# A two-layer attention and expert network: a new planner with timed transfers, other buffers, and the low halves of gated values on POOL from the third dense pass on

## What is computed

```python
x = x + xattn0(layernorm(x), ctx)   # kv = ctx @ W_k.T + b_k; softmax(layernorm((p@kv) @ kv.T))
x = x + ffn0(layernorm(x))          # rms(dense gelu FFN) + rms(top-2 of 8 experts), rms of the sum
x = x + xattn1(layernorm(x), ctx)   # 16 query heads, 4 key heads, rms norms, rotary, causal, @ w_out.T
x = x + ffn1(layernorm(x))          # (silu(x@w_gate.T) * (x@w_up.T)) @ w_down.T
```

## Time and profile before

| what | value |
|---|---|
| median of 3 runs | 2016.03 us (2008.18 to 2016.49) |
| the profiled execution's own time | 2012.14 us |
| its span | 2010.4 us |
| granted TensorE clock, mean | 0.94 |
| PE / DVE / ACT / POOL busy | 1739.0 / 1185.7 / 806.0 / 244.5 us |
| bytes moved by DMA | 409.52 MB, mean 204 GB/s |

### The profile page before, as it was taken

One profiled execution on the slowest core, in us unless ns is written; L12 is line 12 of the kernel. 1 busy time (PEld: TensorE's weight loads), 2 busy tenths in 40 slices (PEclk: granted clock), 3 DMA queues, 4 the chain that ended last, 5 costly groups with the idle time before them and its releaser, 6 DMA issues. The chain is left out here.

```text
span 2010.4 us, 27378 instructions
## 1 busy us (share of the span) xinstructions
PE 1739.0 (86%) x9396; PEld 1369.5 (68%) x9396; DVE 1185.7 (59%) x2583; ACT 806.0 (40%) x1804; POOL 244.5 (12%) x253
## 2 busy tenths in 40 slices
PE   4687897788988998887999899968899769999998
PEld 3566775566888886666767676756676446778887
DVE  6587774373656656877566566648775435553333
ACT  4364552232655653232444365432225435431111
POOL 1233315290000002221000000011310000000000
PEclk9697998998999999998999999989999879999999
DMA  3465459977667788666734553577777025235563
GB/s 102 151 220 204 158 163 347 338 291 277 231 238 274 261 312 329 215 257 224 237 90 123 197 168 117 178 294 267 290 251 231 1 54 156 64 126 201 197 211 104
DMA packets 135464, 409.52 MB, mean 204 GB/s; under 512 B 15136, under 2 KB 29856, under 8 KB 129568
## 3 DMA queue, kind: packets, MB, share of 16 engines
q1 hardware_dynamic: 125200, 372.65, 53.9%
q0 software_dynamic: 10128, 35.13, 4.6%
HBM read 282.95 MB, written 124.78 MB: 203 GB/s over the span
## 5 line engine op out<-in xcount | busy, mean ns | idle before, releaser
L1133 PE MATMUL ps<-xT,gu 128*128 128x512 f32 (+1 forms) x1392 | 538.8, 387 | 88.3 <-DVE act L1611 31.2
L1135 PE MATMUL ps<-xT,gu 128*128 128x512 f32 (+1 forms) x1392 | 515.6, 370 | 0.0
L1134 PE MATMUL ps<-xT,gu 128*128 128x512 f32 (+1 forms) x1392 | 514.7, 370 | 0.0
L1133 PEld LDWEIGHTS ps<-xT,gu 128*128 128x128 f32 x1392 | 271.6, 195 | 149.7 <-DVE act L1611 36.9
L1133 PE MATMUL ps<-wd,hid 128*128 128x512 f32 x604 | 252.6, 418 | 58.4 <-DVE acc L1646 31.8
L1135 PEld LDWEIGHTS ps<-xT,gu 128*128 128x128 f32 x1392 | 270.2, 194 | 44.6
L1134 PEld LDWEIGHTS ps<-xT,gu 128*128 128x128 f32 x1392 | 271.9, 195 | 36.2
L1134 PE MATMUL ps<-wd,hid 128*128 128x512 f32 x604 | 242.8, 402 | 0.0
L1135 PE MATMUL ps<-wd,hid 128*128 128x512 f32 x604 | 242.5, 402 | 0.0
L1338 ACT ACTIVATE hid<-act 128x512 fp32r<-128x512 f32 (+1 forms) x174 | 99.9, 574 | 296.8 <-DVE act L1611 296.6
L1626 DVE TENSOR_TENSOR gu<-raw,gu 128x512 fp32r<-128x512 f32 x188 | 134.7, 739 | 101.5 <-ACT gu L1354 101.0
(11 more groups left out here) (275 smaller groups left out, 2422.0 us busy)
## 6 DMA issues: line engine op xcount, KB each, us to landing
gu<-w_dram SPq DMA_DIRECT2D x160, 512.0 KB, 4.3
raw<-in_ffn_w SPq DMA_DIRECT2D x94, 768.0 KB, 5.6
wd<-w_dram SPq DMA_DIRECT2D x80, 512.0 KB, 5.3
w_dram<-gu SPq DMA_DIRECT2D x32, 1024.0 KB, 8.6
w_dram<-wd SPq DMA_DIRECT2D x32, 512.0 KB, 9.4
QT<-q_dram SPq DMA_DIRECT2D x48, 256.0 KB, 6.9
xg_dram<-zt POOLq DMA_DIRECT2D x23, 512.0 KB, 6.8
x<-xg_dram SPq DMA_DIRECT2D x23, 512.0 KB, 5.9
```

The costliest lines, as they stand in the source:

```text
L1133: mm(out_ap, ah, bh, start=start, stop=False)
L1134: mm(out_ap, ah, bl, start=False, stop=False)
L1135: return mm(out_ap, al, bh, start=False, stop=stop)
```

## The change

**The planner.** Transfers become timed: a table `MOVED` gives each one its SP issues, its KB and an extra latency, and `place` books them on SP (0.35 us an issue) and on a new resource "DMA". All fixed lags go. `on_clock` counts PE's steps slower after little PE work. Several items are cut apart so that each load has its own place (`bload` into `ktload`, `vload`, `woload`, `qload`; `fetch` into `fetch`, `drows`, `mrows`; `cload`, `xsload`, `wostore`).

**The order of passes** becomes (0,0), (0,1), experts, (0,2), (0,3), (1,0) to (1,3), and the slots of `xT` are 0, 1, 1, 0 in layer 0 and 1 - b % 2 in layer 1.

**The buffers.** `xn4` gets memory of its own, so that the first `exp` of a sequence no longer waits for `rowt4`; `aTh` and `aTl` move to a scope that shares with `xn4`, and the first `split` of a sequence has the wait instead. The keys of b = 1, 3 wait only for the last scores of b - 1, the values only for its last values, the queries for the scores two query blocks back.

**The low halves.** From tile 78 on (the third dense pass, the first after the experts; 96 tiles) `low` is a POOL instruction. DVE's `mult` takes the factor 0.5 of the silu and polynomial modes, so ACT's and POOL's halves need none; the number of DVE and ACT operations of `mult` does not change.

```diff
-    TURN = (0, 1, 3, 2)
-    MAIN = [*dense(0, TURN[0]), *dense(0, TURN[1])[:SPLIT], *EXPERTS, *dense(0, TURN[1])[SPLIT:], *dense(0, TURN[2]), *dense(0, TURN[3]), *dense(1, 0), *dense(1, 1), *dense(1, 2), *dense(1, 3)]
+    MAIN = [*dense(0, 0), *dense(0, 1), *EXPERTS, *dense(0, 2), *dense(0, 3), *(tile for b in range(B) for tile in dense(1, b))]
...
+    def on_pool(s):
+        return s >= FIRST["F", 0, 2]
...
-        return b % 2
+        return 1 - b % 2 if f else (0, 1, 1, 0)[b]
...
+    def moves(item):
+        kind, *a = item
...
+        return MOVED.get(kind)
...
         if kind == "low":
-            return [("DVE", 0.6 * width(a[0]) / S)]
+            return [("POOL", 1.25) if on_pool(a[0]) else ("DVE", 0.6 * width(a[0]) / S)]
...
+        def on_clock(t, us):
+            while us > 1e-6:
+                n = int(t / WINDOW + 1e-9)
+                while len(slow) <= n:
+                    slow.append(2 if work.get(len(slow) - 1, 0.0) < (0.38 if slow[-1] == 1 else 0.65) * WINDOW else 1)
...
+                if move:
+                    _, size, extra = move
+                    start, n = reserve("DMA", kind, t, size / 330)
+                    busy["DMA"].insert(n, (start, start + size / 330, None))
+                    t = max(t + size / 270, start + size / 330) + 1.9 + extra
...
-        aTh = sb("aTh", [P, NG, P], F32R, b_scope)
-        aTl = sb("aTl", [P, NG, P], F32R, b_scope)
...
-        xn4 = Pr[:, 0, 0:2, :]
+        b2_scope = ExitStack()
+        aTh = sb("aTh", [P, NG, P], F32R, b2_scope)
+        aTl = sb("aTl", [P, NG, P], F32R, b2_scope)
+        b2_scope.close()
+        xn4 = sb("xn4", [P, 2, D], F32, b_scope)
...
+                elif kind == "low" and on_pool(a[0]):
+                    s = a[0]
+                    if not on_pool(s - 1):
+                        pool.wait_ge(hid_low, nth("low", s - 1))
+                    pool.wait_ge(hid_high, nth("mult", s))
+                    tt(out=hid[:, s % 5, 1, :], in0=act[:, s % 2, :], in1=hid[:, s % 5, 0, :].bitcast(F32), op=ALU.subtract).then_inc(hid_low, 1)
...
-                    if n == 0 and p == 0:
-                        act_.wait_ge(row4_turned, TB * b)
...
+                    if qt == 0:
+                        act_.wait_ge(row4_turned, TB * b)
                     func(aTh[:, :, :], aT[:, :, :], ACT.Copy).then_inc(attn_high, 1)
```

More of the change, by code:

```diff
@@ new lines, in builds_on @@
+            "xtload": lambda: [("xtstore", b, i) for i in range(TB)] + [x_free(b)] + [("xtload", b - 1)] * (b > 1),
+            "top2": lambda: [("logit", B - 1, TB - 1)], "ranks": lambda: [("top2", 2)], "weights": lambda: [("top2", 2)], "before": lambda: [("ranks",)], "blocks": lambda: [("before", 2)],
+            "places": lambda: [("blocks", 3), ("weights",)], "slots": lambda: [("places", 2)],
+            "scatter": lambda: [("slots", 1), ("zero", NB - 1), ("xsload", b)],
+            "xsload": lambda: [("scatter", b - 4)] if b > 3 else [("x1store", n) for n in range(B)] + [("xstore", B - 1, n) for n in range(TB)],
@@ L377, in merge @@
         end, holder, downs, placed = {}, {}, [1], []
-        busy = {"ACT": [], "DVE": [], "POOL": [], "SP": []}
+        busy = {"ACT": [], "DVE": [], "POOL": [], "SP": [], "DMA": []}
         tensor, now, last_of = [], [0.0], {}
         row_turns, row_norms = [], []
+        work, slow = {}, [1]
         def taken(item):
@@ L433, in place @@
                 seen = set()
-                transfer = t
-                for engine, us in steps(item):
+                move = moves(item)
+                for engine, us in steps(item) + ([("SP", 0.35 * move[0])] if move and move[0] else []):
                     if engine == "PE":
-                        t = max(t, now[0]) + us
-                        now[0] = t
+                        t = now[0] = on_clock(max(t, now[0]), us)
                         t += 0.2
+                        tensor.append(item)
                     else:
@@ L495, in two_layers @@
         for b in (pair, pair + 1):
[L496 removed]
+            SIDES += [[[("ktload", b)], [("vload", b)], *[[("woload", b)]] * (b == pair), [("rows", b)]], [[("qload", b, qt)] for qt in range(TB)], value_ticks(b), score_ticks(b)]
     SCHED, ORDERS = merge([main_ticks(), *SIDES])
```

239 lines of the change are left out of this document (123 added, 116 removed).

## The result

| | before | after |
|---|---|---|
| median, us | 2014.30 (2008.18 to 2016.49) | 1914.77 (1911.31 to 1921.50) |
| profiled execution / its span, us | 2012.14 / 2010.4 | 1921.50 / 1919.4 |
| mean granted clock | 0.940 | 0.947 |

The change makes the kernel faster: 0.9515 of the time before, interval [0.9477, 0.9552], or 100 us. The kernel before ran a fourth time beside the change, which is why its median is 2014.30 here and 2016.03 above.

A forecast was written before the change was run, and what follows sets the result against it. The prediction took PE's work plus its waits as the bound, with DVE nearly the bound in the mid work. Its terms, -46 - 6 - 10 + 5 + 8 = -49, took 2012 to 1963 us, range 1922 to 2000.

The forecast's parts named there:

- The first 740 us: Start through the experts: same passes, buffers and bytes, only interleaving planned anew; 0, between minus 15 and plus 15 us.
- rival "more": Planner also wins where transfers are late, 294.3 to 480.4 (13 us) and the burst (15 us): 1935 us; chance 0.15.
- The lone attention: Sequence 2's attention, 1553.6 to 1652.4: its 470 matmuls go among tiles of pass (1,1), 53 us instead of 98.8; minus 46.
- The mid work moved into (1,0): Second pair's mid work runs in pass (1,0) instead of (1,1), with more DMA bytes: plus 8, between minus 15 and plus 30.
- fourth sign: In the profile after, pass (1,0) would show a DMA share over 0.8, and PE waits there.
- joint between layers: 950.8 to 1136.6: new slots free the slot of `xT` one pass earlier; minus 6 of 11 us lost, ends 0 and 11.
- The low halves leave DVE: 96 instructions, 68 us, leave DVE; counts only in the mid work: minus 10 us, between 7 and 20.
- second sign: In the profile after, DVE busy about 68 us less, 1118 plus contention; POOL busy about 370.
- POOL in DVE's way: POOL's low halves hold DVE instructions with two SBUF inputs, in pass (1,0) and mid work: plus 5, ends 0 and 42.
- third sign: In the profile after, splits (DVE, two SBUF inputs) longer than 0.7 us in pass (1,0).
- might not help: Rival that POOL takes back what DVE gives: contention at plus 37 over the forecast, 2000 us; chance 0.07.
- POOL's queue holds PE: Rival: low halves wait behind POOL's mid work items and hold PE's down products; plus 87, 2050 us, slower; chance 0.08.

The follow-up runs named there:

- one list: Against the change with all low halves on DVE: same engine lists, only the 96 low halves issued by POOL; 1909.64 us, against 1901.19 on DVE.

## Why the prediction was right and wrong

**The first 740 us: the step that failed.** The prediction put "0, between minus 15 and plus 15" and said "I see no row that gives it a sign". Measured: minus 44 us (741.1 to 697.1). That is nearly the whole error: the forecast was 49 less, the traces lie 91 apart, and 1963 less 44 is 1919, with a median of 1914.8. The bytes and passes were the same, as said. But the old plan placed weight splits by a fixed lag behind their loads, and the new one by when a transfer can be there. Four runs show that the plan's times set this stretch. Without booked transfers the experts end at 710 instead of 697, without the clock rule at 708. With only the lag gone from the old plan they end at 722 instead of 741, which is 19 of the 44 us; with it put back into the new one, at 762. The new planner alone, with the old order and buffers, ends them at 690. What share each rule has of the 44 us doesn't add up from these runs (13, 11 and 19 us), since each was taken from another plan. Nor do they act in one place: the booked transfers and the clock rule are worth 11.5 us each in (0,1) and cost something in (0,0), and the lag's 19 us lie in (0,0), where the change gains 6.7. So that the planner's times made the gain is shown, and which rule made the 23.3 us of (0,1) stays open.

The row that could have given the sign was there: 294.3 to 480.4 lost 52 us at 311 GB/s, which I took as a limit of the transfers. It was none; the same pass now moves 336 GB/s (54.7 MB in 162.8 us, against 57.9 in 186.1). The rival "more" had this mechanism, "the new planner may also win where transfers are late", with the place right. But I gave it a quarter of the 52 us, 13, where 23.3 came in that pass, and nothing for the start, pass (0,0) and the experts (5.0, 6.7 and 9.0 us).

**The lone attention, minus 46: right.** The stretch is gone, and it is the planner that breaks it up: the old planner with the new order keeps a loss of some 90 us in (1,1), the new planner with the old order and buffers leaves 29.7 of 98.8 us of lone attention. But that pass is then only 24 us shorter with the same matmuls, so the planner alone doesn't bring the whole gain; the order of passes and the buffers have a part in it. The mixed stretch 1392.1 to 1592.4 gives the rate: twelve tiles are 432 matmuls, 97.6 us at 0.226, and the other 970 took 102.7 us, 0.106 each.

**The mid work moved into (1,0), plus 8: inside its ends, at the better side.** The loss of (1,0) grew from 37 to 55 us, with 301 GB/s and a DMA share of 0.82 over 153.3 us, as the fourth sign said; that of (1,1) fell from 91 to 22. Together the two passes lost 128 and now lose 77. Less the 46 of the attention, 5 us were won by this move and the low halves, where the terms had plus 8 and at most 5 less. With the low halves on DVE the two lose 69, so there the move gave 13, near the minus 15 that I had as the end for better spaced transfers.

**The rest of the run as a sum: minus 49 forecast, minus 47 measured.** The terms did not come out one by one. The third pass, where the mid work of the first pair lies, lost 57 us where it had lost 36, with the low halves on either engine, so it is the new plan's or the new order's doing; I had no term for it. The fourth pass, my "joint between layers", lost 31 instead of 42: minus 11, the far end of what I had given, though much of the attention moved into it too (1315 side matmuls in the trace where it had 704), so not all of that need be the joint; with the low halves on DVE it loses 26. (1,2) lost 10 less.

**The low halves leave DVE, minus 10: wrong.** The relief didn't come. On one list, the move cost 8 us, and with a plan of its own 14. The 68 us of low halves did leave DVE, but its busy time fell by 37 (1185.7 to 1148.8), against "about 68" of the second sign. The step took DVE's other instructions as unchanged but for 15 us of contention; they grew by about 30.

**POOL in DVE's way, plus 5: too small, and its rule too narrow.** The relief and this term together were minus 5, and one list showed plus 8; the two can't be parted in time, since a low half on POOL is also 0.6 us longer for those that wait for it. The third sign was right: in pass (1,0) the splits of `gu` have a mean of 821 ns with the change's own plan, and 915 with the low halves on POOL in the list of the version on DVE, against 783 with them on DVE. But I had counted 15 us of DVE's time, and it was about 30, since I counted wide instructions with two SBUF inputs and no others. These grew by 8.6 us; more than half of the growth lay in the small ones of the inverse roots, up to 1.1 us each, and about half of that in ones with a single SBUF input. The Trainium skill ("SBUF — State Buffer", section "Who interferes with whom") says that a `tensor_scalar` can contend with GpSimd too when it enters a 2-port mode, and that the second to issue is blocked in full. The trace agrees, 1.27 us for 0.17, beside a low half that was issued first; in which mode the instruction ran it doesn't show. The Trainium skill's warning that offloading "might not help" ("Perfetto Trace Analysis", section "Optimizing Scalar/DVE Operations"), to which I had given 7%, is what the move showed: 8 us slower by itself, hidden in a change that wins 100 us by other parts.

**POOL's queue holds PE: not in this change.** With the old planner the low halves on POOL cost 40 us, but mostly through late weight loads, and that POOL's queue makes these late isn't shown. In the kernel after POOL waits as before for the mid work, and what waits for a low half waits little. Waits of the whole span:

```profile
POOL qb L1176 <- DVE qb L1914: 69.1, 16, 15.1
...
ACT act L1377 <- POOL hid L1101: 32.8, 24, 1.4
```

The 24 waits of ACT for a low half are at most 1.4 us long.

**The parts don't add.** From the kernel before: the planner minus 77, then order and slots minus 27, then the buffers minus 12, then the low halves on POOL plus 14. But order and slots were worth 14 us beside POOL's low halves, 10 under the old plan; the buffers 12 or nothing. Each step makes a new plan for every engine, and the run with nothing on POOL but a booked 1.25 us shows that such a plan alone can move the time by 18 us. Of the 14 us for the low halves, 8 are the engine, and 6 can't be told from that. It stays open why one plan is better than another there, and how much of the 87 us for the lag is double counting.

## What to carry to other kernels

When a planner's idea of a transfer changes, every stretch that waits for transfers is in play, also those whose bytes and order stay the same: give such a stretch a term from its loss, not zero. Work moved from one engine to another is worth its own time less what it adds to the neighbours, and only where the first engine is on the path; to measure it, keep the lists as they are and change the engine alone, and don't put shorter scratch work in its place. The best version here is the change with the low halves left on DVE, 1900.5 us, 0.9408 of the time before.

## What the runs showed of the hardware

A POOL instruction of 1.29 us also stops DVE's smallest instructions: a `tensor_scalar` on 128x2 with one SBUF input, 0.17 us alone, took up to 1.28 us. So an engine with long chains of small instructions pays for such a neighbour too. In the same kernel the 906 DVE instructions that read PSUM grew by 0.1 us in all, and POOL pieces of 0.50 us instead of 1.3, 143.5 us of them, added only 3.5 us to DVE's busy time. Of 66.9 us of low halves taken from DVE, its busy time gave back about 35.

A pass that moved 311 GB/s, and that I took for bound by transfers, moved 336 with its loads in another order; a single stretch of 28.3 us reached 396:

```profile
697.10:725.40 28.30, 26.68 (x109) 21.03 (x109) 9.27 (x15) 7.90 (x13) 8.36 (x8) 0.95 1.01 396
```
